# Layer 0's edge sum of a two-layer graph network: where four additions of a turn stand in VectorE's list

## What is computed

```
    ex = jnp.exp(att - amax[seg])
    denom = jax.ops.segment_sum(ex, seg, num_segments=S)
    w = ex / denom[seg]
    hsum = jax.ops.segment_sum(w[:, :, None] * val_e, seg, num_segments=S)
    ...
    t_rel = hsum.reshape(n, r, out_dim)
    t = (t_rel * present[..., None].astype(x.dtype)).sum(1) / nrel[:, None]
```

## Time and profile before

| what | value |
|---|---|
| median of 3 runs | 4450.44 us (4441.6 to 4456.38) |
| span of the profiled execution | 4441.9 us |
| layer 0's sum within the span | 2186 to 2693 us |
| VectorE busy, whole span | 2897.9 us (65%) |
| TensorE busy, whole span | 2583.6 us (58%) |
| GpSimd busy, whole span | 2232.5 us (50%) |
| ScalarE busy, whole span | 1649.6 us (37%) |

### The profile page before, as it was taken

The page is one execution under the profiler, slowest core; times in us unless marked ns, Lnnn a source line. Parts: engine busy times, 40 slices in busy tenths (PEclk is TensorE's granted clock), DMA queues, the critical chain, the costliest instruction groups (busy, mean ns, idle before and its releaser), DMA issues. The chain is left out here.

```text
span 4441.9 us, 56033 instructions
## 1 busy us (share of the span) xinstructions
PE 2583.6 (58%) x10078; PEld 1680.6 (38%) x10079; DVE 2897.9 (65%) x5983; ACT 1649.6 (37%) x4237; POOL 2232.5 (50%) x2263
## 2 busy tenths in 40 slices
PE   0499856766666661000388886666356565666653
PEld 0255433434333330000266663443244444444432
DVE  4544445555555556999788886766366566666657
ACT  2244333333333332321166664343233434343443
POOL 4322267777777770000144442221677777777751
PEclk9999978778777775555699998997677777676776
DMA  6366699999999993000377771000666666666652
GB/s 203 121 259 264 258 318 310 315 310 316 313 314 311 315 312 97 0 0 0 116 229 230 228 230 57 18 17 18 154 189 187 193 187 193 186 190 189 190 150 88
DMA packets 577883, 841.19 MB, mean 189 GB/s; under 512 B 137539, under 2 KB 472271, under 8 KB 570917
## 3 DMA queue, kind: packets, MB, share of 16 engines
q0 software_dynamic: 128272, 451.36, 31.9%
q1 hardware_dynamic: 443056, 382.08, 27.5%
q10 hardware_dynamic: 6430, 6.43, 0.5%
HBM read 549.59 MB, written 291.24 MB: 189 GB/s over the span
## 5 line engine op out<-in xcount | busy, mean ns | idle before, releaser
L1911 POOL DMA_INDIRECT g_rows<-x1t,srci x880 | 854.4, 971 | 286.8 <-issue 254.7
L991 POOL DMA_INDIRECT rows<-kv,kvi x880 | 838.3, 953 | 286.7 <-issue 244.4
L1037 PE MATMUL psD<-qs,hot 128*128 x1760 | 698.1, 523 | 257.5 <-DVE prod L1078 202.6
L1078 DVE TENSOR_TENSOR prod<-rows,psD 128x256 f32<-128x256 f32 x880 | 363.9, 418 | 482.7 <-DMA rows<-kv,kvi 375.5
L2065 PE MATMUL g_psM<-g_rows,g_hot 128*128 128x264 f32 x1760 | 572.4, 480 | 76.3 <-DVE g_rows L2183 69.4
L1329 POOL TENSOR_TENSOR wv<-vrows,wgt 128x1024 f32<-128x1024 f32 x110 | 209.8, 1907 | 779.2 <-DVE vhot L1447 778.4
L1037 PEld LDWEIGHTS psD<-qs,hot 128*128 128x128 f32 x1760 | 381.1, 251 | 524.8 <-issue 306.8
L1424 PE MATMUL psM<-wv,vhot 128*128 128x260 f32 x1760 | 431.2, 394 | 77.8 <-DVE run L1443 65.0
L1057 ACT ACTIVATE off<-psB,npiota 128x256 f32<-128x256 f32 x440 | 207.3, 471 | 688.0 <-PE psB L1028 685.6
L2065 PEld LDWEIGHTS g_psM<-g_rows,g_hot 128*128 128x128 f32 x1760 | 391.0, 234 | 170.5 <-issue 92.9
L1424 PEld LDWEIGHTS psM<-wv,vhot 128*128 128x128 f32 x1760 | 323.0, 191 | 185.9 <-DVE run L1443 138.0
(11 more groups left out here) (412 smaller groups left out, 4373.4 us busy)
## 6 DMA issues: line engine op xcount, KB each, us to landing
val_v<-rows SPq DMA_DIRECT2D x220, 512.0 KB, 5.0
vrows<-val_v SPq DMA_DIRECT2D x220, 512.0 KB
sums_v<-g_run SPq DMA_DIRECT2D x110, 528.0 KB, 3.7
g_drow<-drow_v SPq DMA_DIRECT2D x55, 512.0 KB
rows<-kv,kvi POOLq DMA_INDIRECT x880, 5.3
g_rows<-x1t,srci POOLq DMA_INDIRECT x880
g_ndt<-nodeb SPq DMA_DIRECT2D x440, 6.0 KB
hs<-hsort SPq DMA_DIRECT2D x51, 130.0 KB, 2.1
```

Of the source, the lines that this page charges most:

```text
L991: nc.gpsimd.indirect_dma_start(out=rows[:, k], out_offset=None, in_=table, in_offset=bass.IndirectOffsetOnAxis(ap=index[:, i * SLOTS + k:i ...
L1037: nc.tensor.matmul(psD[:, k % 4, 0:cols], hot[:, t % 2, j * P:(j + 1) * P], node[:, ds(blk[t], 1)].rearrange("p o d -> p (o d)"), start=Tr ...
L1078: ins = nc.vector.tensor_tensor(prod[:, k % 4], rows[:, k, 0:D], psD[:, k % 4, 0:D], ALU.mult)
L1911: nc.gpsimd.indirect_dma_start(out=rows[:, i % NBUF, k, 0:ROW1], out_offset=None, in_=dr["x1t"], in_offset=bass.IndirectOffsetOnAxis(ap=v[ ...
```

## The change

The older additions (4 to 7 of the turn before), which stood in a row behind one-hots 0 and 1, are put one by one between VectorE's other instructions: addition 4 behind weighing 0, addition 5 behind one-hots 0, addition 6 behind one-hots 1, addition 7 behind weighing 2. The order of the additions among themselves, and that of the weighings and one-hots among themselves, stay. No instruction and no wait is added or removed, and the other engines' lists are as they were.

```
                 def turn(i, first=False):
-                    for g in range(0, NG, 2):
-                        weigh(dve, nc.vector, i, g)
-                        places(i, g)
-                        if g + 1 < NG - 1:
-                            places(i, g + 1)
-                        if g:
-                            for t in range(4):
-                                add(i, t)
-                        elif not first:
-                            for t in range(4, V8):
-                                add(i - 1, t)
+                    def older(t):
+                        if not first:
+                            add(i - 1, t)
+                    weigh(dve, nc.vector, i, 0)
+                    older(4)
+                    places(i, 0)
+                    older(5)
+                    places(i, 1)
+                    older(6)
+                    weigh(dve, nc.vector, i, 2)
+                    older(7)
+                    places(i, 2)
+                    for t in range(4):
+                        add(i, t)
```

## The result

The changed kernel takes 4510.18 us (median; 4508.71 to 4513.63), the kernel before 4450.81: a ratio of 1.0134, 95% interval 1.0120 to 1.0148. It is 59 us slower. The forecast was 25 us slower.

The account below looks back on a forecast made before the run. VectorE's own list was taken to bound layer 0's sum, 9.16 us a turn. Block 1.32 less saving 0.85 gives 0.47 a turn; times 54 turns, 25 us: 4476 us, 0.57% more, range 4450 to 4510.

Parts of the forecast that it names:

- What the change saves: VectorE's list in layer 0's sum: three self-waits between additions 4 to 7 go, 0.85 us a turn saved.
- The exclusion: GpSimd's weighing and VectorE's weighings and one-hots exclude each other; the block costs 1.32 us a turn.
- Who is first: Behind one-hots 1, VectorE's next weighing starts before GpSimd's first weighing, by 0.07 us.
- Rival 1: GpSimd's first weighing goes before VectorE's weighing 2: net loss 0.99 us a turn, 54 us, 4504; chance 0.22.
- Addition 3: Tile 3 is there at 5.39 us, addition 3 due at 5.46; just fits, if not 0.1 to 0.2 us a turn.
- What is late next: Checks of TensorE's tiles, ScalarE's copies and SyncE's loads under the new order; nothing added to the time.
- The sign that the prediction named last: The forecast falls if TensorE's products hold VectorE's additions.
- rival 2: The block costs less than 0.85 us a turn, the interleaving keeps its gain: 32 us, 4418; chance 0.10.
- rival 3: The block is near 0.85 us, say because GpSimd is held for a part only: no change, 4450; chance 0.11.
- rival 4: VectorE's self-waits cost nothing, so nothing is regained and the block alone gives 71 us, 4522; chance 0.02.

Follow-up runs that it names:

- the third run: The changed kernel, but GpSimd's weighing of group 1 waits for one-hots 0 and no longer for one-hots 1: 4485.80 us, ratio 1.0077.

## Why the prediction was right and wrong

- **What the change saves, 0.85 us a turn: right.** The rows after show the list in the forecast distances, and the run whose GpSimd work only writes keeps 0.75 of it (8.41 for 9.16; the rest is the 0.12 by which weighing 2 was held).
- **The exclusion, 1.32 us: right.** From the start of weighing 2 to addition 0 the forecast had 3.45 us and the turn shown has 3.45 (2314.52 to 2317.97). One instance, the first turn of the trace, was enough to price 54.
- **Who is first: right, by the 0.07 us that was forecast** (2314.52 against 2314.59). Where GpSimd goes first because it is in line early, in the third run, the turn is 9.61, no worse. Rival 1's own case, GpSimd first from a start behind one-hots 1 (10.15), did not come up and wasn't tried.
- **Addition 3: named, not counted.** "It just fits; if not, 0.1 to 0.2 us a turn." It did not fit: it waits for tile 3, 0.30 us of idle where 0.13 was usual, and the turn is 9.77 for 9.63. 8 us.
- **TensorE's clock: the step that failed.** "What is late next" followed TensorE's tiles only as far as the additions that need them, and priced them at full speed, because the stage had run at a granted clock of 0.99. The same lines had the pause in them: tile 1 done early, tile 2 held until GpSimd's product at W + 3.30. I did not write it down as 2.3 us of a still TensorE, where before it had been 0.65, nor ask what the clock would do. It was worth 25 us, as much as the whole forecast. The sign that the prediction named last did come: TensorE's products held the additions, by 1.01 and 1.27 us in the long turn shown.
- **The rivals.** The time lies near rival 1's 4504, but not by its mechanism, so that is chance: VectorE was first in every turn. Rivals 2, 3 and 4 are out; the run whose GpSimd work only writes and the one with the order of the waits changed show that self-waits cost time and can be had back.

## What to carry to other kernels

Before interleaving an engine's waits away, ask what the row of waiting instructions was hiding: here a row of four additions, each with one input in SBUF, was the time in which GpSimd's first weighing could read beside VectorE, and moving even one of them lost until GpSimd was let in sooner. Draw the new schedule for every engine, and write down the longest pause of TensorE in it as a number beside that of the old schedule; a pause that costs little by itself can cost the clock of what follows it. And a gap between dependent instructions has two ways out, other work in it or a shorter wait, of which the second disturbed nobody here.

## What the runs showed of the hardware

- TensorE fell to its lower clock in a loop in which it is busy 7.5 of 9.8 us. With one pause a turn of 2.26 us 15 of 54 turns were touched, with one of 2.15 us 10, with 1.55 us 8; with 1.05 us of work and then 1.37 of rest none, and none in the kernel before with 0.65. The touched turns come regularly, each third or fourth with the pause of 2.26 and mostly each seventh with the two shorter ones, though the pause stands in every turn. Why these turns and not others fall is open.
- GpSimd's weighing and VectorE's two-input instructions do not share but take turns, and the one that started first goes first, even when the starts lie 0.07 us apart (all 54 turns of the changed kernel's loop). Closer than that the recorded starts don't decide: in the run whose GpSimd work only writes, GpSimd went first with a start 0.06 to 0.07 us ahead and VectorE in the one turn in which GpSimd's start was 0.05 ahead. Two-input instructions of VectorE beside GpSimd's fills lost nothing (0.68 us).
- In VectorE's additions the place of a wait among others matters: with the wait for its own predecessor last, the distance fell from 0.70 and 0.72 to 0.62 us; with the one after addition 1 the turn went from 9.16 to 8.90, 14 us over the stage.
